# Expert tiles 3 and 4 as products of rounded parts, and the last two tiles added by one-hot products

## What is computed

```
x = layernorm(x + attention(x))
x = layernorm(x + cross_attention(x, ctx))
# feed-forward, for all 896 tokens
gate_probs = softmax(x @ gate_w + gate_b)
weights, selected = top_k(gate_probs, 2);  weights /= sum(weights)
h = gelu(x @ w1[e] + b1[e])                 # 256 -> 1024
expert_out = h @ w2[e] + b2[e]              # 1024 -> 256
out = sum over the two experts of weights * expert_out
x = layernorm(x + out)
```

## Time and profile before

| | us |
|---|---|
| median of 3 runs | 901.51 (900.63 to 909.01) |
| profiled execution, its own time | 906.78 |
| its span from first to last instruction | 905.0 |
| mean granted clock of PE | 0.981 of 2.4 GHz |
| PE busy | 828.6 (92%) |
| DVE busy | 656.6 (73%) |
| ACT busy | 511.9 (57%) |
| POOL busy | 276.5 (31%) |
| first products of tile 0 begin | 736.8 |
| last product of the last tile's second products begins | 883.95 |

### The profile page before, as it was taken

The page is one execution under the profiler, slowest core; times in us unless marked ns, Lnnn a source line. Parts: engine busy times, 40 slices in busy tenths (PEclk is TensorE's granted clock), DMA queues, the critical chain, the costliest instruction groups (busy, mean ns, idle before and its releaser), DMA issues.

```text
span 905.0 us, 30247 instructions
## 1 busy us (share of the span) xinstructions
PE 828.6 (92%) x12363; PEld 671.4 (74%) x12363; DVE 656.6 (73%) x1348; ACT 511.9 (57%) x1083; POOL 276.5 (31%) x340
## 2 busy tenths in 40 slices
PE   5789989989999999999999999999998889999995
PEld 3567777777777767777777777867776579999993
DVE  5867667767777768786876778776875835688873
ACT  2346555556566556555655665556654443678771
POOL 4143224231612251234214321522250103132331
PEclk9999999999999999999999999999999789999997
DMA  7356545454545545554554555545466655767643
GB/s 216 109 152 174 157 122 157 120 167 120 170 122 150 155 135 155 143 157 131 157 151 134 155 144 162 162 122 157 132 197 244 236 202 151 220 201 209 182 117 93
DMA packets 90948, 143.43 MB, mean 158 GB/s; under 512 B 11362, under 2 KB 79650, under 8 KB 86976
## 3 DMA queue, kind: packets, MB, share of 16 engines
q1 hardware_dynamic: 86592, 132.59, 48.8%
q0 software_dynamic: 4224, 8.95, 3.9%
HBM read 101.60 MB, written 39.81 MB: 156 GB/s over the span
## 4 chain that ended last, share of the span: by engine, by line
PE 61%; DMA 13%; DVE 9%; ACT 8%; SPq 4%; issue 4%; DVEq 0%; POOL 0%; POOLq 0%; ACTq 0%
PE ps L1586 11%; PE ps L1579 10%; DMA k_dram<-k_two 9%; PE ps L1896 9%; PE ps L1660 7%; PE ps L1638 5%; PE ps L1928 4%; PE ps L1602 4%; ACT k_two L1345 3%; SPq L1054 3%; DMA k_st<-k_dram 3%; ACT pT L1372 2%; DVE negmax L502 2%; PE ps L1917 2%; DVE k_two L496 2%
## 5 line engine op out<-in xcount | busy, mean ns | idle before, releaser
L502 DVE TENSOR_REDUCE negmax<-ps 112x1 f32<-112x1500 f32 x121 | 207.4, 1714 | 41.4 <-PE ps L1602 40.6
L1372 ACT ACTIVATE pT<-ps 125x448 f32<-125x448 f32 x384 | 195.9, 547 | 21.1 <-PE ps L1638 17.4
L1203 POOL TENSOR_TENSOR ctx_lo<-ctx_raw,ctx_hi 128x250 fp32r<-128x250 f32 x188 | 130.5, 726 | 230.9 <-DVE ctx_hi L487 230.9
L1638 PE MATMUL ps<-qbd,k_st 98*128 98x112 f16 x1536 | 129.3, 215 | 16.4 <-ACT qbd L1328 6.9
L1638 PEld LDWEIGHTS ps<-qbd,k_st 98*128 98x128 f16 x1536 | 87.1, 99 | 73.9 <-issue 22.8
L496 DVE SCALAR_TENSOR_TENSOR k_two<-ps,bk_sb,k_two 128x500 f16<-128x500 f32 x96 | 70.7, 737 | 88.0 <-ACT k_two L1345 88.0
L1345 ACT ACTIVATE k_two<-ps,bk_sb 128x500 f16<-128x500 f32 x96 | 65.0, 677 | 93.3 <-PE ps L1579 74.9
L1328 ACT COPY v_sb<-ps 125x512 f32<-125x512 f32 x96 | 56.4, 587 | 103.3 <-PE ps L1586 103.3
L1660 PE MATMUL ps<-pT,v_sb 125*17 125x56 f32 x6144 | 93.3, 217 | 8.6 <-issue 8.6
L1660 PEld LDWEIGHTS ps<-pT,v_sb 125*17 125x17 f32 x6144 | 81.4, 100 | 24.9 <-issue 19.4
L1602 PE MATMUL ps<-k_st,qbd 96*112 96x500 f16 x363 | 97.1, 375 | 0.7 <-issue 0.6
(11 more groups left out here) (256 smaller groups left out, 1495.5 us busy)
## 6 DMA issues: line engine op xcount, KB each, us to landing
k_st<-k_dram SPq DMA_DIRECT2D x288, 125.0 KB, 2.6
w_sb<-w SPq DMA_DIRECT2D x25, 1024.0 KB
ctx_raw<-ctx_T SPq DMA_DIRECT2D x48, 500.0 KB, 4.4
k_dram<-k_two SPq DMA_DIRECT2D x96, 250.0 KB, 3.7
xs<-zeros SPq DMA_DIRECT2D x28, 260.0 KB
w_sb<-w POOLq DMA_DIRECT2D x4, 1024.0 KB, 9.4
xg<-xs SPq DMA_DIRECT2D x21, 130.0 KB
a_x<-x_tok SPq DMA_DIRECT2D x8, 128.0 KB, 2.6
```

Source lines behind the costliest of these rows:

```text
L502: V.tensor_reduce(negmax[0:QW], ps[0:QW, BANK_S:BANK_S + CHUNKS, 0:MC], AX.XY, ALU.max, negate=True).then_inc(max_done, 1)
L1203: last = nc.gpsimd.tensor_tensor(ctx_lo[:, k, c2, a], ctx_raw[:, k, c2, a], ctx_hi[:, k, c2, a].bitcast(F32), ALU.subtract)
L1372: nc.scalar.activation(pT[0:MT, (PAIRS * b + p) % 3, TPC * g:TPC * g + TPC], ps[0:MT, BANK_T + n % 2, 0:TPC * QW].rearrange("p (t n) -> p ...
L1638: last = mm(ps[:, BANK_T + n % 2, QW * i:QW * i + QW], k_st[:, j, p, a:a + P], qbd[:, j, p].rearrange("p h s -> p (h s)"), start=True, sto ...
```

## The change

`THREE = 3` is new. Tiles 3 and 4 get `m2_split` too, so that the loops of rounded parts on PE, ACT and DVE run from 3 and not from `EARLY`, and the product for `token_row` moves ahead of `m1(3)`. `tx(5)`, which needs the late table and the last scatter, stands behind `m1(4)` and ahead of `m2_split(3)`. For tile 20 the rounding and subtracting of `h` is cut in two halves. Tile 19 is no longer added by DMA: POOL's last add is that of tile 18, SP waits for 19 adds, and tiles 19 and 20 are both added by one-hot products. For these `y` of both tiles is cut in two parts (`y_parts`), the one-hot matrices are made in fp32r, two sets of them (`hot_step`), and PE makes two products for each set and token tile (`spread`).

```diff
-        token_hot = sb("token_hot", [P, TILES, P])
+        token_hot = sb("token_hot", [P, 2, TILES, P], F32R)
+        y_hi = sb("y_hi", [P, 2, D], F32R)
+        y_lo = sb("y_lo", [P, 2, D], F32R)
...
# DVE
-            xgT_step(4)
-            gate(4)
-            y_step(3)
-            xgT_step(EARLY)
-            gate(EARLY)
-            y_step(EARLY - 1)
...
+            def hot_step(k):
+                for t in range(TILES):
+                    V.tensor_scalar(token_hot[:, k, t], token_row[:], float(P * t + 1), xg[:, (GT - 2 + k) % 2, D:D + 1],
+                                    ALU.add, ALU.is_equal).then_inc(hot_made, 1)
+
+            def y_parts(k):
+                g = GT - 2 + k
+                dve.wait_ge(y_ready, g + 1)
+                V.tensor_copy(y_hi[:, k], y_sb[:, g % 2]).then_inc(y_hi_done, 1)
+                dve.wait_ge(y_hi_done, k + 1)
+                V.tensor_tensor(y_lo[:, k], y_sb[:, g % 2], y_hi[:, k].bitcast(F32), ALU.subtract).then_inc(y_lo_done, 1)
+
+            for g in range(THREE, GT):
                 if g + 1 < GT:
                     xgT_step(g + 1)
                 w2_lo_step(g)
                 if g + 1 < GT:
                     gate(g + 1)
...
+                if g < GT - 1:
+                    h_lo_step(g)
+                    if g > THREE:
+                        y_step(g - 1)
+
+            dve.wait_ge(row_kept, 1)
+            hot_step(0)
+            h_lo_step(GT - 1, slice(0, 4), 0)
+            h_lo_step(GT - 1, slice(4, FT), 1)
+            y_step(GT - 2)
+            y_parts(0)
+            hot_step(1)
             y_step(GT - 1)
+            y_parts(1)
...
# SP
-            sp.wait_ge(added, 16 * (GT - 1))
+            sp.wait_ge(added, 16 * (GT - 2))
...
# POOL
-            for g in range(2, GT - 1):
+            for g in range(2, GT - 2):
                 add(g)
...
# ACT
             for g in range(2, GT):
-                if g >= EARLY:
+                if g >= THREE:
                     w2_hi_step(g)
-                if g == EARLY:
+                if g == THREE:
                     act.wait_ge(row_made, 1)
                     copy(token_row[:], ps[:, BANK_O, 0:P]).then_inc(row_kept, 1)
                 gelu_half(g, 0)
+                if g == GT - 1:
+                    h_hi_step(g, slice(0, 4), 0)
                 gelu_half(g, 1)
...
# PE
-            tx(3)
-            m2(2)
-            m1(3)
-            tx(4)
-            m2(3)
-            m1(4)
-            pe.wait_ge(p_dve, at["late tiles known"])
-            tx(EARLY)
-            m2(EARLY - 1)
-            pe.wait_ge(y_ready, EARLY - 1)
+            tx(THREE)
+            m2(THREE - 1)
+            pe.wait_ge(y_ready, THREE - 1)
             mm(ps[:, BANK_O, 0:P], ones16[:], before16[:], start=True, stop=True).then_inc(row_made, 1)
-            for g in range(EARLY, GT):
+            for g in range(THREE, GT):
                 m1_half(g, 0)
-                if g + 1 < GT:
+                if g + 1 < GT and g + 1 != EARLY:
                     tx(g + 1)
                 m1_half(g, 1)
-                if g > EARLY:
+                if g + 1 == EARLY:
+                    pe.wait_ge(p_dve, at["late tiles known"])
+                    tx(EARLY)
+                if g > THREE:
                     m2_split(g - 1)
...
+            def spread(q, k):
+                for t in (2 * q, 2 * q + 1):
+                    pe.wait_ge(hot_made, TILES * k + t + 1)
+                    pe.wait_ge(y_lo_done, k + 1)
+                    mm(last_sum(t), token_hot[:, k, t], y_hi[:, k], start=False, stop=False)
+                    last = mm(last_sum(t), token_hot[:, k, t], y_lo[:, k], start=False, stop=(k == 1 and t % 2 == 1))
+                    if k == 1:
+                        last.then_inc(hot_done, 1)
+
             carried(0)
+            spread(0, 0)
             carried(1)
-            pe.wait_ge(y_ready, GT)
-            for t in range(TILES):
...
+            spread(0, 1)
+            spread(1, 0)
+            spread(1, 1)
+            for q in (2, 3):
+                carried(q)
+                spread(q, 0)
+                spread(q, 1)
```

More of the change, by code:

```diff
@@ L45 @@
 EARLY = 5
+THREE = 3
 XW = D + 4
@@ L357, in decoder_layer @@
         h_lo_done = sem("h_lo_done")
+        y_hi_done = sem("y_hi_done")
+        y_lo_done = sem("y_lo_done")
         row_kept = sem("row_kept")
@@ L969, in _, with h_lo_step @@
             y_step(2)
-            xgT_step(4)
-            gate(4)
-            y_step(3)
-            xgT_step(EARLY)
-            gate(EARLY)
-            y_step(EARLY - 1)
             def w2_lo_step(g):
                 e = dve.value_load(e_tab[0:1, g:g + 1], min_val=0, max_val=E - 1)
-                dve.wait_ge(w2_hi_done, g - EARLY + 1)
+                dve.wait_ge(w2_hi_done, g - THREE + 1)
                 V.tensor_tensor(w2_lo[:, g % 2], w2_sb[:, bass.ds(e, 1)].rearrange("p a f n -> p (a f) n"),
                                 w2_hi[:, g % 2].bitcast(F32), ALU.subtract).then_inc(w2_lo_done, 1)
-            def h_lo_step(g):
-                dve.wait_ge(h_hi_done, g - EARLY + 1)
-                V.tensor_tensor(h_lo[:, g % 2], hT[:, g % 2], h_hi[:, g % 2].bitcast(F32),
+            def h_lo_step(g, fs=slice(0, FT), half=0):
+                dve.wait_ge(h_hi_done, g - THREE + 1 + half)
+                V.tensor_tensor(h_lo[:, g % 2, fs], hT[:, g % 2, fs], h_hi[:, g % 2, fs].bitcast(F32),
                                 ALU.subtract).then_inc(h_lo_done, 1)
-            for g in range(EARLY, GT):
+            def hot_step(k):
[9 more added lines that the diff above has]
+            for g in range(THREE, GT):
                 if g + 1 < GT:
@@ L993, in _ @@
                     gate(g + 1)
[L994 to L998, removed]
-                    for t in range(TILES):
-                        V.tensor_scalar(token_hot[:, t], token_row[:], float(P * t + 1), xg[:, (GT - 1) % 2, D:D + 1],
-                                        ALU.add, ALU.is_equal).then_inc(hot_made, 1)
+                if g < GT - 1:
[9 more added lines that the diff above has]
+            hot_step(1)
             y_step(GT - 1)
+            y_parts(1)
             def normalise(q):
@@ L1511, in w2_hi_step @@
             def w2_hi_step(g):
-                act.wait_ge(p_dve, at["late tiles known"])
+                act.wait_ge(p_dve, at["early tiles known"] if g < EARLY else at["late tiles known"])
                 e = act.value_load(e_tab[0:1, g:g + 1], min_val=0, max_val=E - 1)
@@ L1515, in w2_hi_step, with h_hi_step @@
                 copy(w2_hi[:, g % 2], w2_sb[:, bass.ds(e, 1)].rearrange("p a f n -> p (a f) n")).then_inc(w2_hi_done, 1)
-            def h_hi_step(g):
-                act.wait_ge(gelu_done, 2 * g + 2)
-                copy(h_hi[:, g % 2], hT[:, g % 2]).then_inc(h_hi_done, 1)
+            def h_hi_step(g, fs=slice(0, FT), half=1):
+                act.wait_ge(gelu_done, 2 * g + 1 + half)
+                copy(h_hi[:, g % 2, fs], hT[:, g % 2, fs]).then_inc(h_hi_done, 1)
             for g in range(2, GT):
-                if g >= EARLY:
+                if g >= THREE:
                     w2_hi_step(g)
-                if g == EARLY:
+                if g == THREE:
                     act.wait_ge(row_made, 1)
@@ L1527, in _ @@
                 gelu_half(g, 0)
+                if g == GT - 1:
+                    h_hi_step(g, slice(0, 4), 0)
                 gelu_half(g, 1)
-                if g >= EARLY:
+                if g == GT - 1:
+                    h_hi_step(g, slice(4, FT), 1)
+                elif g >= THREE:
                     h_hi_step(g)
@@ L1923, in m2_split @@
                 pe.wait_ge(y_ready, g - 1)
-                pe.wait_ge(w2_lo_done, g - EARLY + 1)
-                pe.wait_ge(h_lo_done, g - EARLY + 1)
+                pe.wait_ge(w2_lo_done, g - THREE + 1)
+                pe.wait_ge(h_lo_done, g - THREE + 1)
                 for f in range(FT):
+                    if g == GT - 1 and f == 4:
+                        pe.wait_ge(h_lo_done, g - THREE + 2)
                     for i, (x, w) in enumerate(SPLIT):
```

## The result

Over 20 runs of each, the changed kernel takes 898.55 us in the median (890.88 to 903.23) and the kernel before 905.87 us (896.37 to 917.70). The ratio is 0.9928 with a 95% interval of 0.9907 to 0.9949, so the change takes 4.6 to 8.4 us off, most likely 6.5. The forecast was 7.2 us off. The absolute time of the forecast, 894.3 us with a range up to 897.0, is missed, because the three runs that it started from have a median of 901.51 and twenty have 905.87.

What follows compares the result with a forecast made beforehand. PE alone was taken to bound the expert tiles until 884 us, then tile 19's add and the read-back. Head 0.3 plus tail 6.9 gave 7.2 us off the 901.51 median: 894.3 us, range 892.4 to 897.0.

Steps and rivals of the forecast that it cites:

- I take the 7.2 off the median as it is: Whole kernel: the predicted saving of 7.2 us was subtracted from the three-run median of 901.51 us, giving 894.3 us.
- the head: Start of `m2(2)` to start of `m2_split(18)`: rounded products for tiles 3 and 4 were to save 0.3 us net.
- the tail: Start of `m2_split(18)` to the span's end: earlier read-back and no slow clock were to save 6.9 us.
- the second rival: Tile 5's weights up to 1.7 us later, or tile 18's add up to 1.6: 895.0 to 897.0 us; chance 0.22.
- the slow clock: PE after the read-back: clock at 0.50 for 4.6 us of work; avoiding it was to save 2.3 us.
- the idle gap of 0.95 us: PE ahead of `carried(0)`: idle 0.95 us, where 3.2 us passed before the clock fell, so it would not fall.
- the slower rival: Late rows of tile 5 idle PE; beyond some 3.2 us the clock falls too: about 902 to 911 us; chance 0.03.
- the stall: PE ahead of `m1(5)`: waits 0.8 us for tile 5's weights, with bounds of none and 2.5 us.
- the second of the three arrivals: Rows of tile 5, `xg(5)`, wanted at 769.83 us: in time by some 0.6 us, the wait costing nothing.
- The first, `h_lo(3)`: Arrival ahead of `m2_split(3)`: DVE's `h_lo(3)` ready at 770.05 us, a cost of 0.15 us.
- the weights are in time: Rival ahead of `m1(5)`: tile 5's weights take 4.5 us, the stall goes, 893.5 us; chance 0.18.
- a DVE that bounds the early tiles: Sign of a wrong forecast: PE's first idle in the early tiles ends with `h_lo`.

Runs made afterwards that it cites:

- e10_before_warm80: Kernel before plus 80 unread products of ones on PE behind the last second products: tail 32.59 us against 34.32 before, clock 1.00.
- e9_hold_readback: Changed kernel, but SP issues the read-back of the sums only once `y_lo` of tile 20 is made: tail 34.28 us, against 27.69 in the change.
- e3_before_warm: Kernel before plus 44 unread products of ones on PE behind the last second products: tail 33.52 us; PE still idled 2.40 us.
- e5_expert7: Changed kernel with tiles 5 and 6 loading expert 7's first weights: head 112.70 us against 112.31 in the change, tile 5's load 7.5 us.
- e1_head_only: Kernel before with only tiles 3 and 4 changed to rounded parts: head 112.04, tail 34.32 us, timed ratio to before 1.0007 (0.9964 to 1.0050).
- e6_hot_first: Changed kernel with the first eight one-hot matrices made ahead of `w2_lo(20)`, not behind it: tail 26.14 us against 27.69 in the change, head 112.62.

## Why the prediction was right or wrong

**The absolute time: wrong, by the base.** The step was "I take the 7.2 off the median as it is". That median was of three runs that lie 8.4 us apart. Twenty runs have 905.87, and 905.87 − 7.2 = 898.7, against 898.55 measured. The range took in the bounds of the costs and nothing for the base, although the profiled execution stood 5.3 us above the median on the same page. A range for an absolute time has to carry the spread of the runs that it starts from: single runs of the kernel before lie between 896.37 and 917.70. That 898.7 comes so near is luck in part: the timed ratio gives 6.5 us and leaves 4.6 to 8.4 open, and between the two traces the head and the tail give 6.31, 0.9 less than the forecast.

**The tail: right, and its terms too.** Forecast 6.9, measured 6.63. The add of tile 18 landed 5.76 us after its start (forecast 5.4), the first read after 2.83 us (2.73), PE had no slow clock, `y_lo` wasn't last. The 1.6 us by which the second rival has that add late stand in no run. The second read came earlier than I gave it, so `carried(1)` ran at once at 883.87; `m2_split(20)` gained 0.6 us (its start went from 10.48 to 9.89 us after that of `m2_split(18)`) and not 0.4, but PE then waited for the read-back, so that this was worth nothing. That the slow clock was worth 2.3 us was argued from the earlier trace rows and is confirmed by `e10_before_warm80` (2.1); that the earlier read-back carries the whole of it, by `e9_hold_readback`.

**One reason in it was too wide.** I said the clock wouldn't fall because the idle gap of 0.95 us was shorter than the 3.2 us that had passed before. It didn't fall, but `e3_before_warm` shows that 2.40 us of idle can be enough, with the fall after PE's return. So the point that the slower rival gave, beyond some 3.2 us of idle, lies too high: 2.40 us brought the fall here, 1.16 us (the change, ahead of `carried(0)`) did not.

**The head: the mechanism right, the size off.** The chain does go through tile 5's weights. Forecast 0.3 us less, measured 0.32 more. The term mis-sized is the stall: 0.8 forecast, and 1.13 us of idle, 0.24 more at `tx(5)`, and 0.26 that I had left out, since the first half of products behind an idle takes 2.05 us and not 1.79. The 0.24 is the second of the three arrivals: the rows of tile 5, which I had in time by 0.6 us, landed 3.5 us after their issue in the change, and 2.3 before. The first, `h_lo(3)`, cost nothing where I had 0.15. With the add of tile 2 near it the load of the weights takes anything from 5.8 to 7.5 us to land, so that the size of the stall in one trace is a draw: 1.69 in `e5_expert7` and 1.01 in `e1_head_only`, and the head's spread of 0.7 us comes from there.

**The cause I didn't look for.** I had named the rows and the add in front of the load and the next load beside it, and took the first two as given because the change moves neither. The add was the one that mattered. Holding it costs nothing that the tail shows (26.30, against 26.14 in `e6_hot_first`), and the rival "the weights are in time", at 0.18, is what happens then.

**Ruled out.** The weights' place in memory; a DVE that bounds the early tiles (`m2_split(3)` had its `h_lo` in time in the change); the one-hot rows holding POOL; a steady tile other than 6.62 us.

## What to carry to other kernels

An accumulating DMA that sat ahead of a read-back cost its landing (3.9 us here), the read's landing (2.7) and, as the matrix engine idled over both, the clock of what followed (2.1). The way out was to add the last tiles on the matrix engine and to start the read-back under its last products. Before taking work out of a stretch, look at which load becomes due next and what else is in the DMA engines then, also what nobody waits for. Where GpSimd issues a DMA beside an operation like `w2_lo`, look at which of the two starts first. And take the base of an absolute forecast with its spread.

## What the hardware showed that I had not expected

- Tile 5's 1 MB of weights landed 4.9 and 5.0 us after their issue where the accumulating add of tile 2 was held back, also beside another 1 MB load of the same queue, and in 5.8 to 7.5 us where that add was issued 1.3 to 2.4 us ahead, although it moves only 0.13 MB. In the change's later tiles an add 1.57 us ahead of a load did no such thing (4.9 to 5.7 us).
- An indirect add that starts while a VectorE operation with two SBUF inputs (`w2_lo`, 2.29 us) runs ends 1.43 us after it; one that starts 0.40 us ahead of it takes 1.56 us beside it, and the VectorE operation its 2.29.
- The granted clock fell to 0.50 after an idle of 2.40 us, one microsecond into the next work (`e3_before_warm`), and returned some 3.4 us later; before, it was at 0.50 from 887.2 to 894.0.
- In 14 traces the attention part ended up to 15.7 us apart, while of the 146 us behind it the head repeated within 0.02 us in the old order and within 0.7 with the change's, and the tail within 0.4.
